# Relative tiles walked to and fro with nine buffers of key rows, expert blocks taken from both halves of their list, and the late stack stored straight behind its repacking

## What is computed

```python
x = L0_attn_hidden_states
xn = _layernorm(x, axis=-1)
s = _L0_attn_ref(xn, ...)          # attention, 16 heads of 16
g = _silu(_L0_ffn_ref(xn, ...))    # mix, then 8 experts, two for each token
x = x + s * g
# attention
scores = jnp.einsum('bhqd,bhkd->bhqk', q, k)
dist_idx = pos_l - pos_r + M - 1
pos_emb = dist_emb[dist_idx]
rel_q = jnp.einsum('bhld,lrd->bhlr', q, pos_emb)
rel_k = jnp.einsum('bhrd,lrd->bhlr', k, pos_emb)
scores = (scores + rel_q + rel_k) / jnp.sqrt(jnp.asarray(D, scores.dtype))
# experts: combine holds the two largest router probabilities of a token
h = jax.nn.silu(jnp.einsum('td,edf->tef', flat, w1) + b1)
y = jnp.einsum('tef,efd->ted', h, w2) + b2
out = jnp.einsum('te,ted->td', combine, y)
```

## Time and profile before

| | us |
|---|---|
| median of three runs | 1890.74 |
| the three runs | 1885.74, 1891.82, 1890.74 |
| profiled execution, its own time | 1886.8 |
| its span, first to last instruction | 1885.2 |
| start of the experts' first block | 356.8 |
| last expert block done | 1235.4 |

### The profile page before, as it was taken

The page is one execution under the profiler, slowest core; times in us unless marked ns, Lnnn a source line. Parts: engine busy times, 40 slices in busy tenths (PEclk is TensorE's granted clock), DMA queues, the critical chain, the costliest instruction groups (busy, mean ns, idle before and its releaser), DMA issues.

```text
span 1885.2 us, 35485 instructions
## 1 busy us (share of the span) xinstructions
PE 1579.0 (84%) x12086; PEld 1182.2 (63%) x12086; DVE 1252.6 (66%) x3122; ACT 1041.5 (55%) x2242; POOL 577.4 (31%) x760
## 2 busy tenths in 40 slices
PE   5758640385999988998999899989999999999996
PEld 3324330385888978887888788955555555555553
DVE  6746545360557555655565566768988888997895
ACT  2425320122655534554445355379888888987883
POOL 1352337351010001010111000115263555635546
PEclk9878665698999989999999899999999999999998
DMA  6563426778799889889998988799989999999991
GB/s 212 175 188 113 138 95 217 205 182 277 219 333 331 265 275 371 293 296 347 387 365 280 351 297 296 300 314 317 337 256 332 296 292 324 280 343 283 289 318 46
DMA packets 227284, 510.58 MB, mean 271 GB/s; under 512 B 38208, under 2 KB 84800, under 8 KB 222624
## 3 DMA queue, kind: packets, MB, share of 16 engines
q1 hardware_dynamic: 202144, 410.57, 67.8%
q0 software_dynamic: 23808, 93.54, 14.4%
q10 hardware_dynamic: 1152, 4.19, 0.6%
HBM read 435.11 MB, written 195.82 MB: 335 GB/s over the span
## 4 chain that ended last, share of the span: by engine, by line
PE 45%; DMA 9%; DVE 9%; issue 8%; SPq 4%; ACT 3%; POOL 3%; POOLq 0%; DVEq 0%; ACTq 0%
PE up L1071 9%; PE dn L1083 9%; PE rl L1051 9%; PE pt L1467 7%; DMA scratch_rel<-rel_out 6%; PE sc L1459 4%; PE cx L1480 3%; DVE rel_out L999 3%; SPq L885 2%; DVE probsT L1352 2%; DMA rows<-scratch_sorted 1%; PE wo_ps L1502 1%; DMA late_by_head<-scratch_parts 1%; DVE square L1010 1%; SPq L890 1%
## 5 line engine op out<-in xcount | busy, mean ns | idle before, releaser
L999 DVE TENSOR_TENSOR rel_out<-rl,square 128x1024 f32<-128x1024 f32 x256 | 402.0, 1572 | 271.3 <-PE rl L1051 187.5
L976 ACT COPY square<-rl 128x1024 f32<-128x1024 f32 x256 | 259.2, 1015 | 334.2 <-DVE rel_out L999 226.3
L1309 ACT ACTIVATE square<-square,row_least 128x512 f32<-128x512 f32 x512 | 365.6, 717 | 38.0 <-DVE row_least L1344 37.8
L1344 DVE CUSTOM_DVE_ANT_1 square<-sc,square 128x512 f32<-128x512 f32 x512 | 337.8, 686 | 60.2 <-issue 55.3
L1467 PE MATMUL pt<-ident,square 128*128 128x128 f32 x2048 | 323.0, 281 | 29.2 <-ACT probsT L1316 23.7
L1071 PE MATMUL up<-rowsT,w_b 128*128 128x128 f32 x2272 | 317.1, 287 | 15.9 <-issue 8.0
L1467 PEld LDWEIGHTS pt<-ident,square 128*128 128x128 f32 x2048 | 249.3, 145 | 112.8 <-DVE probsT L1352 42.5
L1083 PE MATMUL dn<-w_b,hid 128*128 128x256 f32 x1136 | 299.5, 393 | 0.0
L1071 PEld LDWEIGHTS up<-rowsT,w_b 128*128 128x128 f32 x2272 | 283.7, 198 | 18.3 <-issue 10.7
L985 ACT ACTIVATE hid<-up,w_b 128x128 f32<-128x128 f32 x568 | 162.2, 372 | 126.4 <-PE up L1071 126.4
L1459 PE MATMUL sc<-late_by_head 96*128 96x512 bf16 x512 | 203.5, 398 | 12.7 <-DVE row_least L1344 10.5
(11 more groups left out here) (197 smaller groups left out, 1690.4 us busy)
## 6 DMA issues: line engine op xcount, KB each, us to landing
scratch_rel<-rel_out SPq DMA_DIRECT2D x256, 512.0 KB, 4.6
square<-scratch_rel SPq DMA_DIRECT2D x256, 512.0 KB, 8.5
w_b<-in_w POOLq DMA_DIRECT2D x71, 1152.0 KB
w_b<-in_w POOLq DMA_DIRECT2D x71, 1028.0 KB
krows_sb<-scratch_stack SPq DMA_DIRECT2D x768, 64.0 KB, 3.4
late_by_head<-scratch_parts SPq DMA_DIRECT2D x384, 64.0 KB, 6.3
scratch_parts<-part SPq DMA_DIRECT2D x96, 128.0 KB
qrows_sb<-scratch_stack SPq DMA_DIRECT2D x192, 64.0 KB, 3.1
```

What stands on the lines that cost most here:

```text
L976: nc.scalar.copy(dst, src).then_inc(s_kc, 1)
L999: nc.vector.tensor_tensor(out[n % SRING][:], rl[r][:].rearrange("p a (b s) -> p (a b) s", s=TILE), square(tile)[:, u * UN:(u + 1) * UN], A ...
L1309: nc.scalar.activation(sm[j][:, i], sm[j][:, i], ACT.Exp, bias=least[:, j, i:i + 1], scale=-1.0, accum_out=es[:, g // 2 % 2, i, 2 * j + g ...
L1344: nc.vector.tensor_tensor_reduce(sm[j][:, i].rearrange("p (c s) -> p c s", c=LT), sc[i % 2][:].rearrange("p (c s) -> p c s", c=LT), rq[j][ ...
```

## The change

`ORDER` lists the tiles: rt runs up for an even lt and down for an odd one, so the last tile of one lt and the first of the next use the same key rows. `RUN` numbers the stretches of tiles with equal rt, 13 for 16 tiles, and key rows are loaded once for each run. The ring of key rows has nine buffers, of which four lie in the room of `late_by_head`, free after the repacking; `used(x)` says after how many k steps piece x may be overwritten. `FIRST_REL` becomes 8. SP issues the first five key pieces between the loads of `late_by_head`, stores the late stack as soon as it is repacked, and then loads key pieces 5 to 8 and the query rows. In the expert blocks, `part_of` maps block jb to place jb // 2 of the list for even jb and to 36 + jb // 2 for odd jb, and `fresh` now compares neighbours in the list.

```diff
-FIRST_REL = 10
+FIRST_REL = 8
-KRING = 5
+KRING = 9
+LATE_SLOTS = 4
+ORDER = [(lt, rt if lt % 2 == 0 else LT - 1 - rt) for lt in range(LT) for rt in range(LT)]
...
-                then(nc.vector.tensor_tensor(fresh_f[:, 2:NBLK], owner_f[:, 2:NBLK], owner_f[:, 0:NBLK - 2], ALU.not_equal))
+                then(nc.vector.tensor_tensor(fresh_f[:, 1:NBLK], owner_f[:, 1:NBLK], owner_f[:, 0:NBLK - 1], ALU.not_equal))
...
+        for late in by_head:
+            room = late[:].rearrange("k h l -> k (h l)").rearrange("k (n x h) -> k n x h", n=LATE_SLOTS // 2, h=BH)
+            kst += [room[:, i] for i in range(LATE_SLOTS // 2)]
...
+        RUN = [sum(ORDER[i][1] != ORDER[i - 1][1] for i in range(1, tile + 1)) for tile in range(TILES)]
+        LAST_OF = {run: tile for tile, run in enumerate(RUN)}
+        RT_OF = {run: ORDER[tile][1] for tile, run in enumerate(RUN)}
+        LOADS = len(LAST_OF) * PIECES
+        NEW_ROW = [tile == 0 or ORDER[tile][0] != ORDER[tile - 1][0] for tile in range(TILES)]
+        def used(x):
+            return LAST_OF[x // PIECES] * UNITS + (x % PIECES + 1) * PER_PIECE
...
             def load_k(x):
-                after(sp, s_kp, (x - KRING + 1) * PER_PIECE)
+                if x >= KRING:
+                    sp.wait_ge(s_kp, used(x - KRING))
...
                 sp.dma_start(by_head[b % 2][:], src).then_inc(s_bh[b % 2], 16)
-            for x in range(KRING):
-                load_k(x)
-            for p in range(PIECES):
-                load_q(0, p)
+                if b < KRING - LATE_SLOTS:
+                    load_k(b)
             sp.wait_ge(s_br, B)
             for i in range(2):
                 dst = t["stack"][2 + i].rearrange("q d l h -> (q d) l h")
                 sp.dma_start(dst, by_row[:, i * TILE:(i + 1) * TILE]).then_inc(s_bs, 16)
+            x = KRING - LATE_SLOTS
+            while x < KRING:
+                load_k(x)
+                x += 1
+            for p in range(PIECES):
+                load_q(0, p)
             sp.wait_ge(s_bs, 16 * 2)
...
-                    x = ((tile + 1) * UNITS + u) // PER_PIECE - 1 + KRING
-                    if u % PER_PIECE == 0 and x < TILES * PIECES:
+                    while x < LOADS and used(x - KRING) <= (tile + 1) * UNITS + u:
                         load_k(x)
...
+            def part_of(jb):
+                return jb // 2 + jb % 2 * EVEN
...
-                return pool.value_load(fresh[0:1, bass.ds(jb, 1)], min_val=0, max_val=1)
+                return pool.value_load(fresh[0:1, bass.ds(part_of(jb), 1)], min_val=0, max_val=1)
```

More of the change, by code:

```diff
@@ L36 @@
 NBLK = TOPK * B * S // TB + NE - 1
+EVEN = (NBLK + 1) // 2
 SPOTS = 8
-FIRST_REL = 10
+FIRST_REL = 8
 LAST_REL = 68
@@ L817, in experts @@
         qst = sb("qrows_sb", [KS, PIECES, PIECE, BH], BF16)
-        kst = [sb(f"krows_sb{i}", [KS, PIECE, BH], BF16) for i in range(KRING)]
+        kst = [sb(f"krows_sb{i}", [KS, PIECE, BH], BF16) for i in range(KRING - LATE_SLOTS)]
         by_head, both = keep["late_by_head"], keep["square"]
+        for late in by_head:
+            room = late[:].rearrange("k h l -> k (h l)").rearrange("k (n x h) -> k n x h", n=LATE_SLOTS // 2, h=BH)
+            kst += [room[:, i] for i in range(LATE_SLOTS // 2)]
         by_row = both[0:KS].bitcast(BF16).rearrange("k a (c h) -> k (a c) h", h=BH)
@@ L880, in load_k @@
             def load_k(x):
-                after(sp, s_kp, (x - KRING + 1) * PER_PIECE)
-                tile, p = x // PIECES, x % PIECES
+                run, p = x // PIECES, x % PIECES
+                if x >= KRING:
+                    sp.wait_ge(s_kp, used(x - KRING))
                 for i, pair in enumerate(PAIRS):
-                    src = t["stack"][tile % LT, PARTS + pair[0], :, p * PIECE:(p + 1) * PIECE]
+                    src = t["stack"][RT_OF[run], PARTS + pair[0], :, p * PIECE:(p + 1) * PIECE]
                     sp.dma_start(kst[x % KRING][i * D:(i + 1) * D], src).then_inc(s_kl[x % KRING], 16)
@@ L903, in sync @@
                 sp.dma_start(dst, by_row[:, i * TILE:(i + 1) * TILE]).then_inc(s_bs, 16)
+            x = KRING - LATE_SLOTS
[4 more added lines that the diff above has]
+                load_q(0, p)
             sp.wait_ge(s_bs, 16 * 2)
-            for p in range(PIECES - 1):
-                load_k(p + KRING)
+            while used(x - KRING) < UNITS:
+                load_k(x)
+                x += 1
             for tile in range(TILES):
@@ L910, in sync @@
                     sp.wait_ge(s_qa, n + 1)
-                    at = (tile % LT * LT + tile // LT) * TILE * TILE + u * UN * TILE
+                    at = (ORDER[tile][1] * LT + ORDER[tile][0]) * TILE * TILE + u * UN * TILE
                     sp.dma_start(t["rel"][:, at:at + UN * TILE], out[n % SRING][:].rearrange("p u s -> p (u s)")).then_inc(s_os[n % SRING], 16)
-                    x = ((tile + 1) * UNITS + u) // PER_PIECE - 1 + KRING
-                    if u % PER_PIECE == 0 and x < TILES * PIECES:
+                    while x < LOADS and used(x - KRING) <= (tile + 1) * UNITS + u:
                         load_k(x)
-                    if tile % LT == LT - 1 and tile + 1 < TILES and u % PER_PIECE == PER_PIECE - 1:
-                        load_q(tile // LT + 1, u // PER_PIECE)
+                        x += 1
+                    if tile + 1 < TILES and NEW_ROW[tile + 1] and u % PER_PIECE == PER_PIECE - 1:
+                        load_q(ORDER[tile + 1][0], u // PER_PIECE)
             rel_stored(sp)
@@ L933, in is_fresh @@
                     return None
[L934 removed]
+                return pool.value_load(fresh[0:1, bass.ds(part_of(jb), 1)], min_val=0, max_val=1)
             def owner_of(jb):
[L937 removed]
+                return pool.value_load(owner[0:1, bass.ds(part_of(jb), 1)], min_val=0, max_val=NE - 1)
             def row_at(jb):
[L940 removed]
+                return pool.value_load(row_of[0:1, bass.ds(part_of(jb), 1)], min_val=0, max_val=ROWS - TB)
             for jb in range(2):
@@ L1030, in relative @@
                 for side, tile, u, r in due(jb, spot):
-                    lt, rt, n = tile // LT, tile % LT, tile * UNITS + u
-                    x = tile * PIECES + u // PER_PIECE
+                    lt, rt = ORDER[tile]
+                    x = RUN[tile] * PIECES + u // PER_PIECE
                     if side == 0:
@@ L1036, in relative @@
                     else:
-                        if u % PER_PIECE == 0 and rt == 0:
+                        if u % PER_PIECE == 0 and NEW_ROW[tile]:
                             pe.wait_ge(s_ql[u // PER_PIECE], (lt + 1) * 16 * len(PAIRS))
```

6 lines of the change are left out of this document (3 added, 3 removed).

## The result

The changed kernel is faster, by a quarter of what I forecast: median 1878.49 us (13 runs, 1867.55 to 1888.01) against 1889.15 us of the kernel before (13 runs, 1881.47 to 1895.08). The ratio is 0.9942, 95% interval 0.9923 to 0.9961, so 11 us instead of 42. On a second chip it was 0.9950 (0.9929 to 0.9972). The time lies above the range of the prediction.

What follows compares the result with a forecast made beforehand. PE was taken as the bound at 12.03 us a block, with late stores losing 61.5 us. Start 439.8 + 14.5 + 698 + 21 lost ends block 67 at 1173.3, 42 us earlier: forecast 1847 us, range 1825 to 1871.

Steps and rivals of the forecast that it cites:

- What bounds the kernel: Experts stage, blocks 10 to 67: PE bound at 12.03 us a block, 61.5 us lost to late stores.
- Weights by halves: Expert weight loads: 7 reloads of one set for 14, none two in a row, 6.3 us of DMA each.
- a share of 0.99 around a single reload: Sign of being wrong: DMA share of 0.99 where one set of expert weights is reloaded.
- Key rows: At the turns: 144 loads of 64 KB saved, losses 6.2, 8.2 and 13.1 us become 5, 5 and 4.
- quiet tile: Tile before each turn: SP has 17 stores and no row load, so enters the turn with its list drained.
- The start: Before block 8: stack store out near 406, key loads in SP's idle time, block 8 starting at 439.8.
- The stall by row loads beside the store: Row loads for blocks 7 to 9 beside the stack's store: the same 11 us stall, moved ahead.
- "slower" rival: Start: every row load beside the stack's store takes 18.6 us, costing 11.4 us each; 1904 us, chance 0.03.
- The list behind the store: SP's 72 row loads behind the stack's store: 34 us to issue, done by 441.
- The sum: To block 67's end: 439.8 + 14.5 + 698 + 21 = 1173.3 instead of 1215.5, 42 us earlier; attention unchanged.
- the one in which the turns and single sets keep most of the loss: Experts stage: SP still needs 3.6 us a unit in turns, 40 us stay lost; 1866 us, chance 0.18.

Runs made afterwards that it cites:

- three-load run on the kernel before: Kernel before, with each piece of key or query rows loaded by three DMAs instead of six and nothing of the change; 1845.52 us, ratio 0.9773.
- three-load run: Changed kernel with the first key loads behind those for the repacking and three DMAs a piece instead of six; 1832.49 us, ratio 0.9718.

## Why the prediction was wrong

**What bounds the kernel.** I read the late stores rightly as the losses, but split them wrongly between weights and SP's list. The three-load run on the kernel before says how it lay: of 61 to 66 us lost against the floor of 693.6 (754.9 and 759.5), 38 to 43 were SP's and 23 the weights'. That is the split with SP's list relieved first; with it untouched, the halves alone saved only 7 to 10. I had also counted five stretches of the earlier trace rows at a DMA share of 0.94 or more, and there are six of ten; but the share was the wrong thing to go by, as the next paragraph shows. The pace was nearly right: 12.03 us a block forecast 712.5 us for the stage from block 8, the floor measured is 708.1.

**Weights by halves: direction right, price of single sets nearly right.** Seven reloads came where forecast, before blocks 9, 17, 20, 25, 34, 37 and 60, and all together cost 6.4 us. I had named a share of 0.99 around a single reload as a sign of being wrong. It is there, 1.00 in blocks 16 and 17, which take 30.4 us. With three loads the same two blocks take 25.5 us, again at a share of 1.00. A full share was no sign of loss.

**Key rows: the step that failed.** "Now SP goes into the tile with its list drained" was to bring the turns down to 5, 5 and 4 us. Against the same blocks at the floor (36.7 us in the three-load run) they kept 8.6, 6.8 and 7.7, 23 us for 14, and the walk to and fro alone moved nothing beyond the noise. The step took it for granted that SP's lag at the start of a turn was part of the loss. But SP had been keeping up in the tiles between turns already (2.3 us for 2.7), so there was next to nothing to drain. The first turn's start shows it (timelines of DVE and SP, two rows of before, then two of after: the add of the unit ahead of the first query loads, and what SP did next):

```profile
624.92 1.22 DVE L999 TENSOR_TENSOR rel_out<-rl,square 128x1024 f32<-128x1024 f32 x1 [0.85 <-PE rl L1051]
627.49 0.52 SPq L912 DMA_DIRECT2D scratch_rel<-rel_out  x1
...
626.83 1.22 DVE L1024 TENSOR_TENSOR rel_out<-rl,square 128x1024 f32<-128x1024 f32 x1 [1.08 <-PE rl L1076]
628.44 3.98 SPq L906 DMA_DIRECT2D qrows_sb<-scratch_stack  x6
```

Before, SP issued that store 1.35 us after the add had ended. Now the store is out and SP at the query loads 0.4 us after it. The quiet tile drained 1.35 us, of the 14 that were short, and the six output buffers were nearly all the credit there was, before and after. The turn's own tile, 15 sets of six loads and 16 stores, needs 3.6 us a unit with or without a quiet tile ahead of it. Three loads instead of six, 1.9 us a unit, took the whole loss away. No run gave more output buffers or put loads on another queue. I had worked out 14 us of shortfall for each turn and then credited the quiet tile with a relief that no row supported.

**The start: the other step that failed.** "Five sets of key loads lie in SP's idle time between the loads for the repacking." The 14.38 us for 30 of them were read where little else was in flight. Between 346 and 366 the four first weight loads and two loads of 768 KB are in flight as well, and there six issues took 16.06 us. That idle time of SP was not free, since the next thing in its list was what DVE and, behind it, PE waited for. It cost 13 us at block 7 in the profile, some 7 in the time. The stall by row loads beside the store came as forecast, 9.28 + 2.52 us for 11, and the fear of the "slower" rival, a stall for every row load, did not come true.

**The list behind the store.** I gave the 72 row loads behind it 34 us to issue; they took 33.01 + 25.61, and the 42 loads after them follow without a gap, so SP's first store of a relative sum left at 498.75, while DVE had added the first unit at 479.4. All six output buffers filled: block 11 took 18.0 us, and blocks 8 to 11 6.8 us more than the floor. With three loads the first store leaves at 465.38 and the loss is gone.

**The sum, corrected** against the profiled execution: start +16.5; the pace -4.4; losses 39.5 for 21, of which the turns +9.0 and block 11, the sets before 17 and 34 and the rest +9.5; attention +4.4, which is its spread. That is +35. Of the rivals, the one in which the turns and single sets keep most of the loss named the right size for the stage, 40 us kept against 39.5 measured. It had SP's 3.6 us a unit right, and the sets beside it, 6.4 us, too high; that the sum fits so closely is luck. The start's loss and attention, which it did not have, put the time above that rival's 1866.

## What to carry to other kernels

A DMA queue that issues in order has a pace of its own: count the issues between two stores, multiply by what one takes (0.47 us here), and set that beside what the engines want, before looking at bytes. Shortening a list in a tile that kept up already gains nothing; shorten the one that doesn't, here by fewer and larger loads. And a queue's idle time ahead of a load that somebody waits for isn't free for other issues, above all while large transfers are in flight.

## What the runs showed of the hardware

- An issue on SP takes 0.42 us and some 0.05 to the next, but it is held up by transfers in flight: one took 11.75 us, 24 behind a store of 6.3 MB took 33.01 and 36.48 us, where 30 with little in flight took 14.16 to 14.38. Of three-load issues, 12 behind that store took 27.61 us, and 9.71 behind the same bytes stored by 16 DMAs, whose own issues took 22.14.
- A row load of POOL passes a large store sooner when the store comes in smaller pieces: landing 6.6 us at the median beside 16 stores with rows of 4 KB, 10.6 beside two with rows of 32 KB.
- The DMA engines moved 387 GB/s in a stretch of 36.7 us at a share of 1.02, more than the 355 to 360 that I had taken for full from the earlier trace rows; the two stretches mix loads, stores and their sizes differently, so a ceiling read from one did not hold for the other.
- Three loads of 192, 128 and 64 KB carry the same bytes as six of 64 KB at half the issue time (1.38 us for 3.09), with no loss in the stage that the profiles show.
- Attention took 646 to 658 us in the fourteen profiles, though its code is the same in all. The four variants of the changed kernel whose turns cost nothing have 656 to 658, so some of their gain may be given back there. Why is left open; it was not tried.
